# The token mixing of a two-layer kernel, from whole-array matmuls to four quarters of TensorE's array

## What is computed

```python
def reference(x, idx, Wc, w12, b12, w3, b3, W, lora_A, lora_B, W_org, down, up, keys, Wq):
    # layer 0: a 64x64 matrix per sequence mixes its tokens
    c = einsum('bct,bcd->bdt', x, Wc[idx])
    x12 = einsum('bsk,mk->bsm', c, w12) + b12
    x1, x2 = split(x12, 2, axis=-1)
    x = x + einsum('bsm,nm->bsn', silu(x1) * x2, w3) + b3
    # layer 1: a linear layer with a low-rank adapter per sequence, then routed experts
    y = x @ W + (x @ lora_A[idx]) @ lora_B[idx]
    base = einsum('bsi,oi->bso', y, W_org)
    coeffs = softmax((mean_s(y) @ Wq.T) @ keys.T / sqrt(128))
    return x + base + einsum('be,bser,ero->bso', coeffs, einsum('bsi,eir->bser', y, down), up)
```

## Time and profile before

| what | before |
|---|---|
| median of 3 runs | 986.02 us |
| the profiled execution's own time | 985.57 us |
| its span, first to last instruction | 983.9 us |
| PE busy | 977.4 us (99%), 4722 passes |
| DVE busy | 791.4 us (80%) |
| ACT busy | 398.8 us (41%) |
| HBM traffic over the span | 85 GB/s |

### The profile page before, as it was taken

One profiled execution on the slowest core, in us unless ns is written; L12 is line 12 of the kernel. 1 busy time (PEld: TensorE's weight loads), 2 busy tenths in 40 slices (PEclk: granted clock), 3 DMA queues, 4 the chain that ended last, 5 costly groups with the idle time before them and its releaser, 6 DMA issues.

```text
span 983.9 us, 12360 instructions
## 1 busy us (share of the span) xinstructions
PE 977.4 (99%) x4722; PEld 806.1 (82%) x4722; DVE 791.4 (80%) x628; ACT 398.8 (41%) x357; POOL 37.0 (4%) x63
## 2 busy tenths in 40 slices
PE   8999999999999999999999999999999999999998
PEld 7888888888888888888898888888888878888886
DVE  3977877998866897778867788779987758896887
ACT  5553553453334333332355545444333443423312
POOL 2600000000000000000100000000000000000001
PEclk9999999999999999999999999999999999999999
DMA  9022044025013101240531210620340140012013
GB/s 356 9 90 104 1 151 190 20 77 183 22 44 129 43 1 64 85 173 1 189 155 43 86 44 8 237 98 28 116 158 1 43 171 1 1 65 86 1 43 129
DMA packets 23273, 84.68 MB, mean 86 GB/s; under 512 B 2722, under 2 KB 6834, under 8 KB 17330
## 3 DMA queue, kind: packets, MB, share of 16 engines
q1 hardware_dynamic: 20962, 76.03, 21.3%
q0 software_dynamic: 2112, 7.36, 1.9%
q10 hardware_dynamic: 144, 0.52, 0.2%
HBM read 75.51 MB, written 8.39 MB: 85 GB/s over the span
## 4 chain that ended last, share of the span: by engine, by line
PE 99%; DMA 0%; SPq 0%; DVE 0%; issue 0%; POOL 0%; POOLq 0%
PE banks L674 31%; PE banks L675 31%; PE banks L676 31%; PE banks L765 3%; PE banks L730 2%; PE banks L748 1%; DMA cond_sb<-cond_t_in 0%; PE banks L778 0%; PE banks L794 0%; DVE r L1051 0%; SPq L556 0%; PE banks L788 0%; SPq L481 0%; PE banks L784 0%; POOL mix L476 0%
## 5 line engine op out<-in xcount | busy, mean ns | idle before, releaser
L674 PE MATMUL banks<-s_hi,t_hi 128*128 128x512 f32 x1344 | 525.5, 391 | 0.0
L675 PE MATMUL banks<-s_lo,t_hi 128*128 128x512 f32 x1344 | 523.3, 389 | 0.0
L676 PE MATMUL banks<-s_hi,t_lo 128*128 128x512 f32 x1344 | 523.0, 389 | 0.0
L674 PEld LDWEIGHTS banks<-s_hi,t_hi 128*128 128x128 f32 x1344 | 252.3, 188 | 56.0 <-issue 4.2
L676 PEld LDWEIGHTS banks<-s_hi,t_lo 128*128 128x128 f32 x1344 | 252.3, 188 | 52.9
L675 PEld LDWEIGHTS banks<-s_lo,t_hi 128*128 128x128 f32 x1344 | 252.4, 188 | 51.6
L1046 DVE TENSOR_TENSOR r<-banks,r 128x1024 f32<-128x1024 f32 x102 | 123.5, 1220 | 52.6 <-PE banks L676 47.8
L927 DVE TENSOR_TENSOR t_lo<-w,t_hi 128x1024 fp32r<-128x1024 f32 x134 | 159.1, 1219 | 1.8 <-ACT t_hi L860 1.8
L841 ACT CAST s_hi<-st 128x2048 fp32r<-128x2048 f32 x40 | 76.5, 1913 | 197.7 <-PE banks L676 145.3
L860 ACT CAST t_hi<-w 128x1024 fp32r<-128x1024 f32 x134 | 135.5, 1048 | 35.5 <-PE banks L676 34.7
L841 ACT CAST s_hi<-r 128x2048 fp32r<-128x2048 f32 (+1 forms) x36 | 63.5, 1769 | 178.4 <-PE banks L676 178.3
(11 more groups left out here) (76 smaller groups left out, 390.7 us busy)
## 6 DMA issues: line engine op xcount, KB each, us to landing
w<-w_up_in SPq DMA_DIRECT2D x16, 1024.0 KB, 4.8
w<-w_base_in SPq DMA_DIRECT2D x10, 1024.0 KB, 4.8
w<-w_down_in SPq DMA_DIRECT2D x8, 1024.0 KB, 5.0
r<-x_t_in SPq DMA_DIRECT2D x8, 1024.0 KB, 6.2
w<-w_lin_in SPq DMA_DIRECT2D x8, 1024.0 KB, 5.3
out_t<-r POOLq DMA_DIRECT2D x14, 512.0 KB, 3.6
we<-w_expin_in SPq DMA_DIRECT2D x10, 512.0 KB, 4.7
r<-x_pairs_in SPq DMA_DIRECT2D x8, 512.0 KB, 9.5
```

The source lines that it names most:

```text
L674: pe.matmul(out, w_hi, x_hi, start=start, stop=False, skip_group_check=True)
L675: pe.matmul(out, w_hi, x_lo, start=False, stop=False, skip_group_check=True)
L676: return pe.matmul(out, w_lo, x_hi, start=False, stop=stop, skip_group_check=True)
```

## The change

The mixing is cut in four per k. Weights are 64 partitions (one sequence, j) by 64 columns of x (q), the moving operand is that sequence's 64x64 matrix, and the result goes to 64 partitions (q) of a bank of sequence j: the four combinations of j and q lie on the four quarters of the array. A pair takes 32 matmuls of 64x64x64 instead of 8 of 128x128x128. `mix` loses its zero blocks and its memsets. The two banks of a pair now each hold one sequence, so ACT's copy reads and writes rows of 64 elements instead of 128.

Three things are moved in the order of work. For h = 0, ACT makes `t_hi` of product 0 after `s_hi` of product 0 instead of after pair 1's copy, and DVE makes `s_lo` before `t_lo`. For h = 1, DVE does two of its four weight sums before `s_lo` of product 0 and two after it.

```diff
-        mix = sb("mix", [P, PAIRS, P])
+        mix = sb("mix", [P, PAIRS, S])
...
-                    copy(mix[rows, bass.ds(i * 2 + parity, 1), rows].rearrange("p a m -> p (a m)"),
+                    copy(mix[rows, bass.ds(i * 2 + parity, 1), :].rearrange("p a m -> p (a m)"),
...
             def mixing(h):
...
-                    out = banks[:, bank:bank + 2, :].rearrange("p a (k m) -> p (a k) m", m=P)
                     for k in range(K):
-                        last = pe.matmul(out[:, k, :], x_pair(c)[:, k * P:(k + 1) * P], mix[:, c, :], start=True, stop=True)
+                        for q in range(2):
+                            for j in range(2):
+                                rows, cols = slice(j * S, (j + 1) * S), slice(q * S, (q + 1) * S)
+                                last = pe.matmul(banks[cols, bank + j, k * S:(k + 1) * S],
+                                                 x_pair(c)[rows, k * P + q * S:k * P + (q + 1) * S],
+                                                 mix[rows, c, :], start=True, stop=True, skip_group_check=True)
                     last.then_inc(mixed_full, 1)
...
-            pe.wait_ge(mix_zeroed, 2)
...
                     dst = r[:, base:base + 2, :].rearrange("p a (k n) -> p (a k) n", n=TN)
-                    src = banks[:, 2 * (c % 4):2 * (c % 4) + 2, :].rearrange("p a (k m) -> p (a k) m", m=P)
-                    act.copy(dst[:, :, c % 4 * P:(c % 4 + 1) * P], src).then_inc(mixed_copied, 1)
-                    if c == 1 and h == 0:
-                        t_split(-1, 0)
+                    dst = dst[:, :, c % 4 * P:(c % 4 + 1) * P].rearrange("p k (j m) -> p j k m", m=S)
+                    src = banks[:, 2 * (c % 4):2 * (c % 4) + 2, :].rearrange("p j (k m) -> p j k m", m=S)
+                    act.copy(dst, src).then_inc(mixed_copied, 1)
                     if c == PAIRS // 2 - 1:
                         s_split(phase_of(h, "up0", 0))
+                        if h == 0:
+                            t_split(-1, 0)
...
-            dve.memset(mix[0:S, :, S:P], 0.0).then_inc(mix_zeroed, 1)
-            dve.memset(mix[S:P, :, 0:S], 0.0).then_inc(mix_zeroed, 1)
...
-                dve.tensor_copy(mix[S:P, c, S:P], cond_sb[S:P, bass.ds(v, 1), :].rearrange("p a m -> p (a m)")).then_inc(
+                dve.tensor_copy(mix[S:P, c, :], cond_sb[S:P, bass.ds(v, 1), :].rearrange("p a m -> p (a m)")).then_inc(
...
+            s_split(0)
             t_split(-1, 0)
-            s_split(0)
...
-                    for what in t_sums_beside(n):
+                    sums = t_sums_beside(n)
+                    for what in sums[:2]:
                         t_sum(*what)
                     if i == 6 and h + 1 < HALVES:
                         s_split(n + 1)
+                    for what in sums[2:]:
+                        t_sum(*what)
```

More of the change, by code:

```diff
@@ L326, in build @@
         wq_loaded = sem("wq_loaded")
-        ones_made, mix_zeroed = sem("ones_made"), sem("mix_zeroed")
+        ones_made = sem("ones_made")
         consts_made, masks_made = sem("consts_made"), sem("masks_made")
```

## The result

| what | before | after |
|---|---|---|
| median of 5 runs | 986.02 us (985.60 to 987.99) | 995.68 us (994.76 to 996.16) |
| ratio after / before, 95% interval | | 1.0095 [1.0083, 1.0106] |
| the profiled execution's own time | 985.57 us | 996.16 us |
| its span | 983.9 us | 994.5 us |

The change costs 1% where 0.7% less was forecast, and the time lies 5 us above the top of the predicted range. First the page after: PE's line, the granted clock in 40 slices, TensorE's instruction queue (q8), and the chain that ended last by engine and line.

A forecast was written before the change was run, and what follows sets the result against it. TensorE was taken to bound the kernel, busy 977.4 of 983.9 us. Gains of 2.3 and 4.9 us less 0.1 for small edits took 7.1 off 985.57: 978.5, or 979.0 us as the median; range 977.5 to 990.5.

The forecast's parts named there:

- the 56 that the strips and row halves of before let one expect: Mixing: four overlapping quarter passes of 64 columns need 56 ns, half of a whole-array pass's 111 ns.
- the 1.05 that I took: Mixing: a pair in quarters takes 1.05 us, from about 15 ns a pass and 0.1 us for waits between pairs.
- the rival of row halves that do not overlap: Mixing: row halves and strips together do not overlap, a pair takes 3.6 us, +14.3 us a half, 1014 us; chance 0.03.
- a feeding limit at 20 to 29.5 ns: Mixing: the sequencer limits passes; at 29.5 ns 987 us, at 20 ns a gain of about 5 us; chance 0.18.
- the code does not arrive: Mixing: TensorE waits for instruction blocks fetched through full DMA queues; 993 us at worst, 990 in the middle; chance 0.16.
- My 5.4 us: Mixing: each wait for a new instruction block lasts 5.4 us, as a load of 8 KB took under full queues.
- The clock: First half: PE's wait for x from 11.8 to 14.4 us drops the clock to 1.2 GHz, 983 us; chance 0.07.
- The chain on ACT and DVE: Second half: copies, `s_hi` and `s_lo`, not TensorE, set product 0's start at 503.3 instead of 508.17 us, -4.9 us.

The follow-up runs named there:

- order_only: The kernel before with only the moved splits and weight sums, the mixing left as whole-array matmuls: 985.71 us, ratio 0.9998.
- quiet_queue: The changed kernel with the first stage's three later weight loads (3 MB) issued only after the first mixing: 990.77 us, ratio 1.0054.
- shift_blocks: The changed kernel with one warm-up matmul less and 24 tiny ones more, 92 more recorded instructions ahead of the mixing: 995.52 us, ratio 1.0099.
- late_pairs: The kernel before with the moved orders and quarters only for pairs 3, 6 and 7 of the second half: 984.01 us, ratio 0.9982.
- row_halves: The changed kernel with two row-half matmuls per k and no column halves, 256 passes a half instead of 512: 986.96 us, ratio 1.0012.

## Why the prediction was wrong

**What held.** The change of order cost nothing (order_only), and ACT's copies take 1012 ns on average against 1014. Four quarters do overlap: fed, passes start about 15 ns apart (14.8 over 177 of them, 15.0 over 126 in quiet_queue), some 59 ns for four, close to the 56 that the strips and row halves of before let one expect. A lone pair in quarters takes 1.09 us, start to start (499.47 to 500.56), against the 1.05 that I took. So neither the rival of row halves that do not overlap nor that of a feeding limit at 20 to 29.5 ns came in. (By its own 1.89 us a pair that rival's price in the first half was +0.8, not +0.3: 8 x 1.89 = 15.1 against 14.34; it changes nothing here.) On feeding the Trainium skill, TensorE: Matmul & The Clock Gate, section "Wait — 56ns, not 53.3ns?", has no start closer than about 25 ns; these traces go against that between different quarters, with those 177 passes 14.8 ns apart.

**The step that failed** is "I take about 15 ns and 0.1 us for the waits between pairs, 1.05 us a pair": a distance of two passes, right while the code is there, was used as the rate of 512 of them. Measured, with the stops, a pair took 2.6 us in the first mixing (20.59 / 8) and 2.0 in the second (16.36 / 8). The rival "the code does not arrive" is what happened, in the way that it was written: runs of about 128 passes, stops of microseconds, a packet of the instruction queue before each end. I gave it 0.16 because no fetch showed as a stop before. But before, no block of 256 records behind record 193, in the first mixing, lasted less than 13 us; the row said nothing of one that lasts 1.85 us. shift_blocks and quiet_queue show the cause: a stop moves with the place in the code and shortens with the queues' load. The Trainium skill's Runtime: NRT & Kernel Launch, section "Instruction fetch mechanics", names a store of 2048 instructions and two blocks; the stops every 126 passes agree with the second alone. No run was made to test that just one block is on its way, but the traces can be counted. In all thirteen, the instruction queue brings one packet more than there are blocks of 256 records begun behind record 449, and the packet with a block's code never starts earlier than 42 records before PE enters the block ahead of it. PE enters a new block 1.2 us after its packet's end at the earliest. So the code for a block is asked for about when the block before it is entered, as the theory has it.

**The sizes within that rival.** From start to start a block takes 6.1 to 6.3 us under full queues and 3.7 to 4.0 in the second mixing. My 5.4 us came from a load of 8 KB under full queues, a fair stand-in for the delivery but not for the 1.3 to 1.6 us from the packet's end to the first pass. For the first mixing I gave this rival an end at 25.4 us, and it was 28.6, 0.6 of it from the later beginning. The second I put at +3.5 or, with queues that empty, at -2: it was +2.15. There, even empty queues deliver a block in no less than whole-array passes take for the same work (3.7 us against 126 / 4 x 111 ns = 3.5).

**The clock** was a rival of its own with 0.07, started by a wait for x. It came as a companion of the stops instead: in the changed kernel, with each stop of 2.5 us and more, the clock fell to 1.2 GHz for 3.4 us, late in the stop or within 0.6 us behind it (with the first stop, 2.7 of the 3.4 us fell on work), and with those of 1.50 and 0.48 us it did not. Within the first mixing this cost little, since the next block was not there anyway: the 126 passes from 21.45 took 3.53 us at the lower level and 2.09 at the upper one (quiet_queue, from 19.68), and the next start hung on the packet. It cost 1.3 us on product 0. How much of the second mixing's 2.15 us is the clock's and how much the delivery's, no experiment separates; all three of its starts follow a packet's end by 1.3 to 1.6 us, which speaks for the delivery.

**The range** ended at 990.5, in the middle of the code rival, whose worse end I had worked out at 993. A case of 0.16 had thus been cut in half; and its two prices were treated as separate from the clock's, though here it was the stops that brought the clock down. Both together gave 995.7.

**The chain on ACT and DVE** that was to decide the second half never did: in the changed kernel `s_lo` is ready at 517.3 (from 515.01), and PE's last pass ends at 518.6. In late_pairs, too, product 0 starts behind the last pass, at 506.37, but there `s_lo` is ready only 0.4 us earlier, at 506.01: in that kernel TensorE alone could not bring much more.

## What to carry to other kernels

Cutting a matmul into tiles buys array time with instructions: count them, divide by the block (here 256), and ask whether each block lasts as long as its successor's delivery, some 4 us with idle DMA queues and 6 with full ones. Where it does not, tile only a burst of some 64 to 128 passes, with longer instructions on both sides and away from heavy transfers, as late_pairs did: its shortest block lasts 5.3 us. Price a rival by what it sets off as well: here a stop of 2.5 us and more also lowered the clock for what came next.

## What the runs showed of the hardware

- TensorE has the block of 256 instructions at work and one more at best, by the count in all thirteen traces. The stops put down to issue in the views of waits stand in the mixing, but for one of 0.5 us in the first passes of product 0 behind it (shift_blocks).
- One packet of 16 KB takes 1.0 us in the median of the changed kernel (0.9 to 1.4), and after a stop the engine goes on 1.3 to 1.6 us after its end, whether the queues are full or not.
- Quarter passes of 64x64x64 in fp32 start 14.8 to 15.0 ns apart at 2.4 GHz and 26.5 at 1.2. Going over from whole-array to quarter passes and back costs about 0.1 us each way: in late_pairs 0.21 us lie between the last whole-array start and the first quarter one (499.26 to 499.47), and again between the first two starts of whole-array passes behind the quarters (500.56 to 500.77), where 0.11 is usual.
- The clock's lower level lasted 3.4 us each time in the changed kernel, but 17.1 us in shift_blocks, with much the same stops in its first mixing, and 13.7 us (18.6 to 32.3) after a wait of 0.96 us in one execution of row_halves. Ten other executions of row_halves show nothing of the kind in their times. What decides between them stays open.
